# Adding the odd pairs' tile by an accumulating DMA instead of on VectorE, with the steps of four queues set in a new order

## The reference, cut to what matters

```
x = x + 0.5 * ffn(layernorm(x))     # 8 experts of 128 -> 512 -> 128, top 2 of 8 per token, silu
x = x + mixer(layernorm(x))         # two passes of a selective scan, then a chunked memory
x = x + 0.5 * ffn(layernorm(x))     # the same experts
```

```
xz = u @ in_w.T + in_b ; xm, res = split(xz)      # 256 channels each
xm = silu(conv4(xm)) ; delta = softplus(...) ; B, C = 16 states each
h  = h * exp(delta * A) + (delta * xm) * B        # over 256 steps, 16 states per channel
y  = sum over the 16 states of h * C  +  xm * D_ssm
out = (y * silu(res)) @ out_w.T + out_b
```

## Time and profile before

| | |
|---|---|
| median of 3 runs | 1654.6 us (1653.92 to 1655.49) |
| the profiled execution | 1653.32 us, span 1651.5 us |
| DVE busy | 1391.1 us, 84% of the span |
| PE busy | 1316.8 us, 80% |
| ACT busy | 1251.1 us, 76% |
| GpSimd busy | 649.9 us, 39% |
| DMA that GpSimd issues (software queue) | 38.5% of 16 engines' span |
| DMA that SyncE issues (hardware queue) | 21.6% |

### The profile page before, as it was taken

How to read it: one execution, slowest core, us unless ns; L and a number is a source line. 1 busy time by engine, 2 the same in 40 slices (tenths; PEclk the granted TensorE clock), 3 DMA queues, 4 the chain that set the end, 5 groups by cost and what they waited for, 6 DMA issues and landing times. The chain is left out here.

```text
span 1651.5 us, 29004 instructions
## 1 busy us (share of the span) xinstructions
PE 1316.8 (80%) x8642; PEld 1185.8 (72%) x8642; DVE 1391.1 (84%) x2151; ACT 1251.1 (76%) x2596; POOL 649.9 (39%) x681
## 2 busy tenths in 40 slices
PE   7977568878888688878888688878888787668778
PEld 6967457767778686867777686868877686457668
DVE  3368999989989888989989888989889889988842
ACT  3489658978888787977889787978889688549722
POOL 1212434273625446273624536263534533242220
PEclk9989668989999799999989899997989799779889
DMA  5446347675666667675666667665666665465631
GB/s 189 121 94 139 77 86 158 139 181 133 161 143 145 143 134 179 151 173 119 155 152 139 158 141 182 141 165 117 149 158 142 163 143 106 83 139 117 151 90 45
DMA packets 144230, 227.02 MB, mean 137 GB/s; under 512 B 13648, under 2 KB 79440, under 8 KB 143952
## 3 DMA queue, kind: packets, MB, share of 16 engines
q0 software_dynamic: 39424, 123.76, 38.5%
q1 hardware_dynamic: 104656, 101.41, 21.6%
HBM read 90.90 MB, written 25.17 MB: 70 GB/s over the span
## 5 line engine op out<-in xcount | busy, mean ns | idle before, releaser
L983 ACT ACTIVATE dA<-delta,A 128x255 f32<-128x255 f32 x1024 | 425.7, 495 | 5.3 <-DVE hs L1353 4.4
L1359 DVE TENSOR_TENSOR_SCAN hs<-dA,b_r 128x512 f32<-128x512 f32 x256 | 297.7, 1202 | 13.1 <-PE b_r L671 10.4
L1353 DVE TENSOR_TENSOR_SCAN hs<-dA,dbu 128x1024 f32<-128x1024 f32 x128 | 292.9, 2288 | 16.3 <-ACT dA L983 10.4
L558 PE MATMUL b_out<-w2s,hT 128*128 x1680 | 243.7, 293 | 13.9 <-ACT ys L905 7.8
L1371 DVE TENSOR_TENSOR G<-hs,b_r 128x1024 f32<-128x1024 f32 x192 | 233.4, 1216 | 22.0 <-PE b_r L682 13.9
L544 PE MATMUL b_h<-xsT,wst 128*128 128x128 f32 x1680 | 245.8, 294 | 5.2 <-ACT hT L913 5.2
L558 PEld LDWEIGHTS b_out<-w2s,hT 128*128 128x128 f32 x1680 | 223.1, 206 | 22.0 <-issue 20.9
L854 ACT ACT_TABLE_LOAD x182 | 233.5, 1283 | 3.9 <-PEq L1762 0.7
L544 PEld LDWEIGHTS b_h<-xsT,wst 128*128 128x128 f32 x1680 | 228.5, 210 | 7.5 <-issue 7.0
L671 PE MATMUL b_r<-prm,scaled 128*128 128x128 f32 x1024 | 171.6, 298 | 64.4 <-ACT scaled L999 28.8
L999 ACT ACTIVATE scaled<-duT,dtT 128x256 f32<-128x256 f32 x512 | 217.1, 501 | 0.3
(11 more groups left out here) (181 smaller groups left out, 2220.2 us busy)
## 6 DMA issues: line engine op xcount, KB each, us to landing
wst<-w_dram SPq DMA_DIRECT2D x242, 256.0 KB
acc<-G POOLq DMA_DIRECT2D x96, 512.0 KB
odd<-G POOLq DMA_DIRECT2D x96, 512.0 KB
xsort<-sorted SPq DMA_DIRECT2D x70, 192.0 KB
results<-ys SPq DMA_DIRECT2D x70, 192.0 KB, 3.1
odd<-xd POOLq DMA_DIRECT2D x32, 256.0 KB
xin<-x_dram SPq DMA_DIRECT2D x8, 256.0 KB
sorted<-ys SPq DMA_DIRECT2D x2, 960.0 KB, 7.3
```

The source lines that it names most:

```text
L558: last = mm(Y[:, i % CH * D:(i % CH + 1) * D], hT[i % NH][:, c, :], w2s[:, e, c, :], start=c == 0, stop=c == HC - 1)
L983: last = do(dA[j % 4][:, d, k, 1:], delta[b][:, k, 1:], ACT.Exp, scale=A[:, k, s:s + 1])
L1353: V.tensor_tensor_scan(flat(hs[j % 2]), flat(dA[j % 4]), flat(dbu[n % 2]), 0.0, ALU.mult, ALU.add)\
L1359: V.tensor_tensor_scan(hs[j % 2][:, d, :, :].rearrange("p h t -> p (h t)"), dA[j % 4][:, d, :, :].rearrange("p h t -> p (h t)"), R[u % 2][ ...
```

## The change

A new function `merge` on GpSimd waits until the additions of pairs 6 and 7 have landed and issues one more accumulating DMA, which adds the whole tile `odd` to `acc`. In `gate_y` the two waits, the 1024-column addition and its drain go, and one wait for the new DMA takes their place. The new step is called `w0` in GpSimd's order.

```diff
 def gate_y(g, i):
     q, b = 4 * g + i, i % 2
-    dve.wait_ge(*landed(q, 6))
-    dve.wait_ge(*landed(q, 7))
-    V.tensor_tensor(acc[b][:, :, :, :], acc[b][:, :, :, :], odd[b][:, :, :, :], ALU.add)
-    dve.drain()
+    dve.wait_ge(q_sum, (q + 1) * 16)
     wait(dve, q_omm, q)
...
+def merge(g, i):
+    q, b = 4 * g + i, i % 2
+    pool.wait_ge(*landed(q, 6))
+    pool.wait_ge(*landed(q, 7))
+    Q.dma_start(flat(acc[b]), flat(odd[b]), accum_op=ALU.add).then_inc(q_sum, 16)
...
+    elif name == "w":
+        if tail:
+            merge(*tail)
...
 def finish():
     one, two = slice(0, HALF), slice(HALF, TILES)
     f = (LAST, xb, ob, GROUPS - 1, False)
+    merge(GROUPS - 1, 3)
     ffn_root(LAST, one)
```

In the table all four queues change. Two entries, slot D on GpSimd and on DVE:

```diff
-"froot skip sc0 sc1 sc2 a2 sc3 sc4 fkeep a3 sc5 sc6 sc7 a4 ga0 ...
+"w0 froot skip sc0 sc1 sc2 a2 sc3 sc4 fkeep a3 sc5 sc6 sc7 a4 ga0 ...
-"b0 fstats s0 s1 fnorm b2 g0 flog ftop g1 fplace s2 g2 s3 gate g3 b4 s4 fweights g4 s5 low g5 ...
+"b0 fstats s0 s1 fnorm b2 g0 flog ftop g1 fplace s2 g2 s3 gate g3 b4 s4 g4 s5 fweights low g5 ...
```

More of the change, by code:

```diff
@@ L112 @@
     "tensor": (
[4 rows of a table removed]
[8 rows of a table added]
     ),
     "scalar": (
[4 rows of a table removed]
[6 rows of a table added]
     ),
     "vector": (
[4 rows of a table removed]
[6 rows of a table added]
     ),
     "gpsimd": (
[4 rows of a table removed]
+        "w0 skip a2 a3 a4 a5 a6 a7",
+        "froot w0 skip sc0 sc1 sc2 a2 sc3 rms a3 sc4 sc5 sc6 sc7 rs a4 ga0 fkeep ga1 ga2 ga3 a5 ga4 ga5 ga6 "
+        "ga7 a6 a7",
+        "w0 skip rms rs a2 lnx a3 rmsx a4 a5 a6 a7",
+        "w0 froot skip sc0 sc1 sc2 a2 sc3 sc4 fkeep a3 sc5 sc6 sc7 a4 ga0 ga1 ga2 ga3 a5 ga4 ga5 ga6 ga7 a6 "
+        "a7",
     ),
```

## The result

The changed kernel takes 1662.8 us (median of 20 runs, 1655.7 to 1671.6), the kernel before took 1654.6 beside it: a ratio of 1.0046, 95% interval [1.0033, 1.0059]. It is 8.2 us slower where 10.3 us less was forecast, and 0.8 us above the upper end of the forecast range. The profiled execution has a span of 1662.8 us, 11.3 above before's. A span is about 1.8 us shorter than the time of the same execution.

The account below looks back on a forecast made before the run. VectorE bounds slots A and C, GpSimd's chain the second half of B and D. Five groups at -1.7, groups 0, 6, 7 at -1.9, -1.7, -1.1, end +2.9: -10.3, so 1644.3 us; range 1629 to 1662.

Parts of the forecast that it names:

- I leave 0.4 us: Slots D: `fnorm` 2.1 us late behind the merge's wait; idle time before `flog` takes most, 0.4 us remains.
- I take 0.3: Slots D: `xm` 2.0 us late behind `F24`, mostly covered by the gather wait and the 1.29 us saved; 0.3 us remains.
- about -1.9: Group 0, with three gates, no scatter in B and no gathers in D: about 1.9 us saved.
- if the cover is gone: Slots B: late `uT` costs nothing under 4.5 us of cover, up to 2.9 us without that cover.
- some 18: Slots A and C: removing the addition saves 1.29 us of VectorE time a slot, 18 us counted for them.
- Slots A and C: The gate's wait for the merge costs 0.15 us in A, 0.2 in C, leaving -1.1 us for each slot.
- the end: Behind the last slot the merge stands before the root, 3.7 us later; net cost +2.9 us (2.4 to 3.7).
- the shrunk wait before `flog`: Sign in slots D: `fnorm` starts about 2 us later and the wait before `flog` shrinks by about as much.
- turn it slower: Rival: extra ScalarE work makes `uT` and `xm` late in slots B and D; up to 24 us slower, 1678 us; 16%.
- the wait for the gathers at the start of slots C: Sign: VectorE's wait there should be near 4.5 us instead of 3.24.
- the wait for `dA` at the ends of slots D: Sign of error: VectorE waiting for `dA` at the end of slots B and D.
- waits before `yg`: Sign: some tenths of a us before `yg` in slots A and C; over 1 us would show an error.

Follow-up runs that it names:

- the old orders: Order table of the kernel before, with only the merge put in: 1671.8 us; gates of slots A and C also one step later: 1668.1; root also ahead of merge: 1649.8.
- all three costs repaired: Changed kernel with the root ahead of the merge (slot D, end), slot D's ScalarE row as before, and `uT` ahead of `d6` in slot B: 1636.2 us, 0.9898.
- the kernel before with the root's wait: Kernel before, no merge, GpSimd waiting for pairs 6 and 7 ahead of the root in slot D and at the end: 1658.1 us, 1.0018.

## Why the prediction was wrong

**The failed step: slots D, "I leave 0.4 us" and "I take 0.3".** The delay was read rightly: the text had the merge's landing wait end at 603, 6.6 us after `g7` at 596.4, and the trace has 6.5; `xn` was forecast 2.1 us late and is 2.56. What failed was the cover. The idle time before `flog` was taken as room of 3.04 us into which most of the delay fits. But the product for which `flog` waits is itself made from `xn`, through PE and ScalarE, so only what is left over in that path is room: about 1 us in the old orders. And in the new ones the room is 1.26 us. The text has `fgate` "behind the same number of pieces", but PE's row has 9 before it in the old order of slot D and 8 in the new one. The root's place costs 2.1 us in each of groups 1 to 5 (943.8 less 933.3), not 0.4. Of these, 1.08 are seen at `lg` (0.75 beside the kernel before) and 0.63 still at `fsum` behind the gathers; slots A are 1.0 us longer and slots B 0.4, with a wait for PE before `G` of 0.77 us in a slot A against 0.03; how the root's place brings that about is not shown. The ScalarE row, sized at 0.3 against the same gather wait and the same saved 1.29 us, costs 1.3 (6.6 over five groups). Its 0.3 stood for the late `xm` alone. The wait for a decay step, which the forecast named only as a sign of being wrong, had no price, and it is 2.78 us.

**The second: group 0, "about -1.9".** `uT` behind `d6` was costed at nothing, with up to 2.9 us "if the cover is gone". For groups 1 to 5 that was right: slots B grow by 4.4 us, `xa` waits no more, and `uT` first brings back only 0.3 us a group. Group 0 has no gathers to wait for. The same text says that it has no scatter in B, and still gave it the cover. Beside the kernel with `uT` first, and counted from the end of slot A in each trace, PE's projection from `uT` starts 3.0 us late, and the three slots are 6.2 us longer. That is twice the delay, and the other half is PE's own slowness: its projection took 8.0 us instead of 5.0. Over the projection PE's granted clock was 0.60 in the mean, mostly at its lower level of 1.2 GHz, from 164.7 to 172.4; in the other kernel it was 1.00, 2.4 GHz throughout, from 161.0 to 166.2. The next two fences are these stretches, columns as in the earlier trace rows.

```profile
164.70:172.40 7.70, 7.64 (x25) 6.42 (x25) 0.00 (x1) 1.28 (x2) 3.98 (x4) 0.60 0.41 87
```

```profile
161.00:166.20 5.20, 5.16 (x27) 4.53 (x27) 2.87 (x3) 4.34 (x7) 2.63 (x3) 1.00 0.88 178
```

Ahead of the fall PE had stood idle for 2.8 us, waiting for `uT`. The other slots B of the changed kernel say more. PE stands idle for 2.8 us at this place in each of groups 0 to 6. The clock over the projection was then 0.62 in groups 0, 3 and 4, 0.75 in groups 2 and 6, and 1.00 in groups 1 and 5. With `uT` first there is no such idle time, and the clock was 1.00 in all seven. So each fall came behind the idle time, but the same idle time did not always bring one. Group 5 of the changed kernel, at full clock:

```profile
1111.15:1116.18 5.03, 5.03 (x26) 4.49 (x27) 0.01 (x1) 1.25 (x1) 4.38 (x5) 1.00 0.86 242
```

In the kernel before with only `d6` late, group 0 has 2.6 us of idle time, a clock of 1.00, and slots that are only 1.4 us longer.

With these terms in place of the forecast's the sum is -10.3 + 5 * (2.1 - 0.4) + 5 * (1.3 - 0.3) + 6.2 + 5 * 0.3 = +10.9 us, beside 11.3 in the traces and 8.2 in the medians. That it fits so well is luck. It leaves out three larger terms that nearly cancel: the saving is worth 26.8 us and not some 18; the merge costs 22 us in the old orders (1627.8 to 1649.8), where the forecast had 2.6; and the other order edits, which the forecast took to be worth nothing, are worth some 13. With all three costs repaired the kernel is 18.4 us faster than before.

**Slots A and C.** The wait for the merge was sized at 2.6 us in all (8 * 0.15 + 7 * 0.2) and is 7.9 at `yg`. The wait before `x` grows by 4.7 more; it comes with the gate's later place and not with the merge's landing, as the runs with the old orders show. The merge lands 5.2 us after its issue in the median (4.5 to 6.6), near the short end of the forecast's 4.86 to 8.75. By the Trainium skill ("DMA: Bandwidth & Descriptors", section on the anatomy of one DMA on the GpSimd path), 2.0 us plus the bytes over 436 GB/s, an estimate for this tile is 3.2 us. The trace disagrees with that estimate, and the short row did better. The wait is not the whole price: of the merge's 22 us in the old orders, 9.5 are there without the gate's wait for the landing, and the forecast had nothing for them.

**What held.** VectorE's busy time (1352 forecast, 1351.2), 214 table loads, ScalarE's busy time (1292, 1295.7), GpSimd's chain from the first scatter to the last gather (30.8 us in slots B and 29.4 in slots D, 30.7 and 29.7 before), the end (+2.9, +2.7), the shrunk wait before `flog`. A table load beside a decay step still costs its 1.28 us alone: 161.44 + 1.28 is 162.72, and `dA` starts at 162.73. One rival had part of the mechanism: the late `uT` and the new ScalarE row "turn it slower" is about half of what happened (7.0 and 8.9 us of the 31.6 that the three repairs gave alone). Its prices of 2.9 us in each slot B and 2.0 in each slot D were too high for groups 1 to 5 (0.3 and 1.3) and too low for group 0 (6.2). No rival had the root's place. The forecast held them all off with covers counted more than once. Of the signs, the wait for the gathers at the start of slots C should have grown to 4.5 us; it is gone in groups 1 to 5, since slots B became longer by more than it. Of those named as proof of an error, the wait for `dA` at the ends of slots D did appear (2.78 us), and three of the 32 waits before `yg` are over 1 us (1.98 at most). The one for `b_w` there (1.49 us) says nothing: before it was 1.55 us in the mean.

## What to carry to other kernels

An idle time covers a new delay only if what ends it does not hang on the delayed work, and only once: add up all delays that lay claim to the same idle time and the same saving before any is costed at nothing, and do it for the first and last groups by themselves. Alone in the kernel before, the root's wait cost 3 us and the late `d6` 4. In the kernels with the merge, putting the root first was worth 16 and 18 us, and putting `uT` ahead of `d6` 7. A wait for a transfer's landing goes behind the small work that others wait for: exchanging root and merge turned 1.0046 into 0.9958.

## What the runs showed of the hardware

The first instruction of the norm's root, 128x4 on GpSimd, takes 2.08 to 2.14 us in slots D of the kernel before and of the one with the root ahead, where a scan runs on VectorE, and 0.52 in the changed kernel, where VectorE mostly stands still. The second takes 1.03 to 1.04 us in all of them. A scan is not all that it takes, though: in the kernel before with the root's wait two roots that lie within a scan take 0.20 us for the first instruction (at 232.32 and 980.50). What decides it is not shown. So the changed kernel's root, which starts 5.2 us later than before's (7.62 against 2.45 in the mean), is done only 3.6 us later (9.25 against 5.70).

Without VectorE's addition of 1024 columns GpSimd's chain of scatters and gathers in slot B is 1.2 us shorter, of which 0.6 are two waits for VectorE; the forecast had 0.2 for this, and 0.6 at most.
